# Pair loops of five layers written out, and one floor and reciprocal for both activation maxima of a quantised feed-forward

## What is computed

```python
x = x + cross_attention(ln(x), ctx)      # 16 heads, 256 keys
x = x + causal_attention(ln(x))          # 16 heads
x = x + quantised_ffn(ln(x))
x = x + single_head_cross(ln(x), ctx)
x = x + causal_attention(ln(x))          # 16 heads
x = x + experts(ln(x))                   # 32 routed and a shared one
```

```python
scale = 127.0 / clip(max(abs(x), axis=-1), 1e-5)
xq = clip(round(x * scale), -128, 127) / scale      # for x, and again for silu(gate) * up
```

## Time and profile before

| | us |
|---|---|
| median of 3 runs | 1245.86 |
| range of the runs | 1245.34 to 1248.54 |
| the profiled execution | 1246.51 |
| its span | 1244.7 |
| TensorE busy | 1181.4 |
| VectorE busy | 814.7 |
| ScalarE busy | 643.4 |
| GpSimd busy | 559.6 |

### The profile page before, as it was taken

One profiled execution on the slowest core, in us unless ns is written; L12 is line 12 of the kernel. 1 busy time (PEld: TensorE's weight loads), 2 busy tenths in 40 slices (PEclk: granted clock), 3 DMA queues, 4 the chain that ended last, 5 costly groups with the idle time before them and its releaser, 6 DMA issues.

```text
span 1244.7 us, 30235 instructions
## 1 busy us (share of the span) xinstructions
PE 1181.4 (95%) x9751; PEld 933.6 (75%) x9760; DVE 814.7 (65%) x1805; ACT 643.4 (52%) x1394; POOL 559.6 (45%) x833
## 2 busy tenths in 40 slices
PE   6899999989997778989998999999999999999998
PEld 4688888767775546777777888888888888888886
DVE  4688888867776888868899764444444544444444
ACT  4777677645555887545555434434333434343432
POOL 2144444667774444568885223232323233323232
PEclk9999999999999999999999999999999999999999
DMA  8200000000001001200000233333333433333331
GB/s 274 73 27 17 17 17 8 2 1 2 0 0 35 1 1 42 62 26 2 0 0 28 89 106 125 107 102 118 108 107 109 140 103 116 116 106 103 118 107 62
DMA packets 34041, 80.13 MB, mean 64 GB/s; under 512 B 4416, under 2 KB 12096, under 8 KB 33984
## 3 DMA queue, kind: packets, MB, share of 16 engines
q1 hardware_dynamic: 32800, 78.09, 19.4%
q10 hardware_dynamic: 1184, 1.31, 0.3%
HBM read 77.03 MB, written 2.36 MB: 64 GB/s over the span
## 4 chain that ended last, share of the span: by engine, by line
PE 78%; POOL 6%; DVE 6%; issue 5%; ACT 3%; DMA 0%; DVEq 0%; POOLq 0%; ACTq 0%; SPq 0%
PE ps L2448 10%; PE ps L2449 10%; PE ps L2447 10%; PE ps L444 5%; PE ps L2530 5%; PE ps L2529 5%; PE ps L2531 5%; PE ps L459 3%; POOL Kbd L1419 3%; PE ps L432 3%; PE ps L1095 2%; POOL Sm L1412 2%; PE ps L260 2%; PE ps L1065 1%; PE ps L1086 1%
## 5 line engine op out<-in xcount | busy, mean ns | idle before, releaser
L2816 POOL TENSOR_TENSOR sw<-sg,wb 128x512 f32<-128x512 f32 x136 | 176.5, 1298 | 386.6 <-ACT sg L2640 352.7
L2719 DVE TENSOR_TENSOR a<-sw,ps 128x512 f32<-128x512 f32 x136 | 93.5, 687 | 224.8 <-POOL sw L2816 224.5
L2645 ACT ACTIVATE ah<-a 128x512 fp32r<-128x512 f32 x136 | 85.9, 632 | 290.8 <-DVE a L2719 261.6
L2447 PE MATMUL ps<-Hh,wh 128*128 128x512 f32 x544 | 215.3, 396 | 0.0
L2448 PE MATMUL ps<-Hl,wh 128*128 128x512 f32 x544 | 214.4, 394 | 0.0
L2449 PE MATMUL ps<-Hh,wl 128*128 128x512 f32 x544 | 214.4, 394 | 0.0
L2723 DVE TENSOR_TENSOR al<-a,ah 128x512 fp32r<-128x512 f32 x136 | 95.6, 703 | 62.4 <-ACT ah L2645 59.3
L760 ACT ACTIVATE Pr<-ps,mx 128x256 f32<-128x256 f32 x256 | 104.2, 480 | 61.0 <-DVE mx L629 56.4
L2447 PEld LDWEIGHTS ps<-Hh,wh 128*128 128x128 f32 x544 | 101.9, 187 | 24.9 <-issue 0.8
L2449 PEld LDWEIGHTS ps<-Hh,wl 128*128 128x128 f32 x544 | 101.8, 187 | 24.9
L2448 PEld LDWEIGHTS ps<-Hl,wh 128*128 128x128 f32 x544 | 101.9, 187 | 23.6
(11 more groups left out here) (238 smaller groups left out, 2448.8 us busy)
## 6 DMA issues: line engine op xcount, KB each, us to landing
wb<-token_weights SPq DMA_DIRECT2D x64, 512.0 KB, 3.6
raw<-in_ew SPq DMA_DIRECT2D x66, 384.0 KB, 3.0
cT<-in_ctxT SPq DMA_DIRECT2D x16, 256.0 KB, 2.7
cx<-in_ctxT SPq DMA_DIRECT2D x15, 256.0 KB, 2.8
X<-in_x SPq DMA_DIRECT2D x1, 1536.0 KB, 7.2
wqkv<-in_wqkv SPq DMA_DIRECT2D x2, 768.0 KB, 5.2
raw3g<-in_wg SPq DMA_DIRECT2D x1, 1024.0 KB, 5.3
raw3u<-in_wu SPq DMA_DIRECT2D x1, 1024.0 KB, 7.4
```

The source lines that it names most:

```text
L2447: eng.matmul(ps[:, bank, :], wh[:, u, w], HhT[:, c, cols], start=(c == 0), stop=False)
L2719: eng.tensor_tensor(a[:, tt, :], sw[:, tt, :], ps[:, UB[tt], :], ALU.mult).then_inc(m_a, 1)
L2816: eng.tensor_tensor(sw[:, tt, :], sg[:, tt, :], wb[:, u, tt * UT:(tt + 1) * UT], ALU.mult).then_inc(m_sw, 1)
```

## The change

Five pair loops become Python loops: the same steps in the same order, i is a number, and there is no loop instruction. In the feed-forward the two maxima of a buffer lie side by side in one tile (column 0 for a, column 1 for h). `scale_both(i)` computes the floor and the reciprocal of the second maximum of pair i and of the first one of pair i+2 with one instruction each. It stands after the row maximum of pair i+2, where `front1` had its own, and what followed `amax2`'s maximum directly is gone. At the first two steps and at the last two it works on one column. Readers of the scales wait on the joint semaphores.

```diff
@@ long_pipeline, routed_pipeline, both pairs()
-    with eng.Fori(0, (NPAIR - 4) // 2) as j:
+    for j in range((NPAIR - 4) // 2):
...
-    with eng.Fori(0, (NPAIR - 6) // 2) as j:
+    for j in range((NPAIR - 6) // 2):
...
-        with eng.Fori(0, 5) as j:
+        for j in range(5):
...
-        with eng.Fori(0, 2) as j:
+        for j in range(2):
@@ quantised_ffn
-    am = sb("am3", [P, 2, 1]); ac = sb("ac3", [P, 2, 1]); sc = sb("sc3", [P, 2, 1]); dq = sb("dq3", [P, 2, 3])
-    am2 = sb("am32", [P, 2, 1]); ac2 = sb("ac32", [P, 2, 1]); sc2 = sb("sc32", [P, 2, 1]); dq2 = sb("dq32", [P, 2, 1])
+    am = sb("am3", [P, 2, 2]); ac = sb("ac3", [P, 2, 2]); sc = sb("sc3", [P, 2, 2])
+    dq = sb("dq3", [P, 2, 3]); dq2 = sb("dq32", [P, 2, 1])
@@ vector
-        def front1(i, u):
+        def row_max(i, u):
             eng.wait_ge(ln_h, base + i + 1)
-            eng.tensor_reduce(am[:, u, :], h[:, u, :], AX.X, ALU.max,
+            eng.tensor_reduce(am[:, u, 1:2], h[:, u, :], AX.X, ALU.max,
                               apply_absolute_value=True).then_inc(f_am, 1)
...
+        def inner_max(i, u):
+            eng.wait_ge(f_a, 2 * i + 2)
+            eng.tensor_reduce(am[:, u, 0:1], a[:, u, :], AX.X, ALU.max,
+                              apply_absolute_value=True).then_inc(f_am2, 1)
+
+        def scale_both(i, u):
+            c = slice(0 if within(i, 0, last) else 1, 2 if within(i, -2, last - 2) else 1)
+            if within(i, -2, last - 2):
+                eng.wait_ge(f_am, i + 3)
+            reach(eng, f_am2, i + 1)
+            reach(eng, f_dq, i + 1)
+            reach(eng, f_dq2, i - 1)
+            eng.tensor_scalar(ac[:, u, c], am[:, u, c], 1e-5, 1.0 / 127.0, ALU.max, ALU.mult).then_inc(f_ac, 1)
+            eng.wait_ge(f_ac, i + 3)
+            reach(eng, f_ar, i - 1)
+            reach(eng, f_r, i + 1)
+            eng.reciprocal(sc[:, u, c], ac[:, u, c]).then_inc(f_sc, 1)
...
-                amax2(i, u)
+                inner_max(i, u)
...
-                front1(i + 2, u)
+                row_max(i + 2, u)
+            if within(i, -2, last):
+                scale_both(i, u)
@@ scalar, round2
-            eng.wait_ge(f_sc2, i + 1)
+            eng.wait_ge(f_sc, i + 3)
...
-                           scale=sc2[:, u, :]).then_inc(f_ar, 1)
+                           scale=sc[:, u, 0:1]).then_inc(f_ar, 1)
@@ gpsimd, scale2
-            eng.wait_ge(f_ac2, i + 1)
+            eng.wait_ge(f_ac, i + 3)
...
-            eng.tensor_tensor(dq2[:, u, :], wsc[:, 2:3], ac2[:, u, :], ALU.mult).then_inc(f_dq2, 1)
+            eng.tensor_tensor(dq2[:, u, :], wsc[:, 2:3], ac[:, u, 0:1], ALU.mult).then_inc(f_dq2, 1)
```

More of the change, by code:

```diff
@@ L1512, in quantised_ffn @@
     f_g = sem(n + "g"); f_u = sem(n + "u"); f_sg = sem(n + "sg"); f_a = sem(n + "a")
-    f_am2 = sem(n + "am2"); f_ac2 = sem(n + "ac2"); f_sc2 = sem(n + "sc2"); f_dq2 = sem(n + "dq2")
+    f_am2 = sem(n + "am2"); f_dq2 = sem(n + "dq2")
     f_ar = sem(n + "ar"); f_at = sem(n + "at"); f_ate = sem(n + "ate"); f_o = sem(n + "o"); f_y = sem(n + "y")
@@ L1655, in mul @@
                                      op0=ALU.mult, op1=ALU.mult).then_inc(f_a, 1)
[L1657 to L1663, removed]
-            eng.wait_ge(f_ac2, i + 1)
-            eng.reciprocal(sc2[:, u, :], ac2[:, u, :]).then_inc(f_sc2, 1)
         def body(i, u):
@@ L1686, in first @@
         def first():
-            front1(0, 0)
+            row_max(0, 0)
+            scale_both(-2, 0)
             ln_dve(eng, L, 1, 1)
@@ L1691, in first @@
             ln_dve2(eng, L, 1, 1, f_r)
-            front1(1, 1)
+            row_max(1, 1)
+            scale_both(-1, 1)
             ln_dve(eng, L, 2, 0)
@@ L1766, in round1 @@
             eng.nop(nofuse=True)
-            eng.tensor_scalar(r[:, u, :], h[:, u, :], sc[:, u, :], ROUND, ALU.mult, ALU.add).then_inc(f_r, 1)
+            eng.tensor_scalar(r[:, u, :], h[:, u, :], sc[:, u, 1:2], ROUND, ALU.mult, ALU.add).then_inc(f_r, 1)
         def scales(i, u):
@@ L1772, in scales @@
             eng.nop(nofuse=True)
-            eng.tensor_scalar(dq[:, u, :], wsc[:, :], ac[:, u, :], None, ALU.mult).then_inc(f_dq, 1)
+            eng.tensor_scalar(dq[:, u, :], wsc[:, :], ac[:, u, 1:2], None, ALU.mult).then_inc(f_dq, 1)
         def scale2(i, u):
-            eng.wait_ge(f_ac2, i + 1)
+            eng.wait_ge(f_ac, i + 3)
             reach(eng, f_y, i - 1)
-            eng.tensor_tensor(dq2[:, u, :], wsc[:, 2:3], ac2[:, u, :], ALU.mult).then_inc(f_dq2, 1)
+            eng.tensor_tensor(dq2[:, u, :], wsc[:, 2:3], ac[:, u, 0:1], ALU.mult).then_inc(f_dq2, 1)
         def add_x(t, u):
```

## The result

In the same rounds the kernel before took 1246.66 us (median, 1245.34 to 1249.52) and the changed one 1240.77 us (1239.60 to 1242.19). The ratio is 0.9947, with a 95% interval of 0.9936 to 0.9958: 0.5% faster, more than the 0.3% that can be told from no change. The profiled execution has a span of 1239.0 us against 1244.7, so 5.7 us less; between the medians it is 5.9. The sum had 7.3.

The account below looks back on a forecast made before the run. TensorE was taken to bound all layers but the feed-forward, judged by VectorE with ScalarE close behind. Savings of 1.2 + 1.1 + 4.6 + 0 + 0.4 = 7.3 us gave 1238.6 us; range 1235.2 to 1242.4.

Parts of the forecast that it names:

- Cross attention and layer 2, 1.2 and 1.1 us: Twelve looped pairs in each layer, written out, save 0.10 us per pair in cross attention and 0.09 in layer 2.
- rival A: Outside the feed-forward TensorE hides the loops, so only 4.6 us go: 1241.2 us; 12%.
- rival C: Code loading shows: 44 kB per pair waited for in 12 cross pairs, 28 us, partly; near 1250 us or above; 3%.
- Feed-forward, 4.6 us: Feed-forward: over 13 periods the last second sg starts 4.6 us earlier, at 4.76 us per pair instead of 5.12.
- ScalarE's floor of 4.76 us: Feed-forward: ScalarE's steps per pair sum to 4.76 us, just below VectorE's written-out period of 4.85, and set the pace.
- Part 2: Feed-forward: one floor and one reciprocal for both maxima, worth 0 to 1.1 us within the 4.6.
- no gap ahead of VectorE's product ends with sg: Sign for the feed-forward: VectorE should show gaps ahead of the product that end with sg; two pairs take 9.5 us.
- the reserve: Feed-forward: 1.3 us left before the later joint scale would hold up ScalarE's ar.
- rival D: TensorE's half-clock stretches at joints between layers appear or go, up to 1.7 us each: 1236.9 or 1240.3 us; 12%, split.
- Layer 5, +0.4 us: Fifth layer, 10 looped pairs: 7.73 us each looped, 7.69 written out, so 0.4 us saved; range 0 to 2.6.
- this way to fail: The prediction fails if the measured written-out pairs were short for their place at a layer's end, not for being written out.

Follow-up runs that it names:

- VectorE's nudge: Changed kernel plus one extra one-element addition on VectorE ahead of hn, once, at pair 4 of layer 5; one pair took 8.69 us and the alternation went on.
- GpSimd's nudge: Changed kernel plus one extra one-element GpSimd addition, once, at pair 4 of layer 5; ratio 0.9940, layer 5 at 7.807 us per pair.

## Why the prediction was right, and where it was not

*Forecast and time.* 1238.6 us was forecast and 1240.77 measured, inside 1235.2 to 1242.4; faster, as was thought likely. Of the 2.2 us between them, 1.4 are in the saving (7.3 against 5.9 between the medians), and 0.8 is that the medians of before differ between the two sets of runs.

*Cross attention and layer 2, 1.2 and 1.1 us.* Measured 1.3 and 1.1, right to 0.1 us in both. In layer 2 that is partly luck: the looped pairs alternate between 7.84 and 7.69, 0.07 us per pair and not 0.09, and the remaining 0.36 us come from the first looped interval (8.05, now 7.69), which the prediction didn't look at. A written-out pair at the end of a stage, in which TensorE was full in both forms, was a sound measure of what the loop costs, and rival A (TensorE hides it) fell. Instruction loading shows as 1.05 MB on queue 8 (0.51 before) and as 2 and 3 GB/s beside TensorE rows that are full, and the intervals are those of the pair that was measured ahead of time: rival C fell too.

*Feed-forward, 4.6 us.* Measured 4.7. ScalarE's floor of 4.76 us, added up from five steps of the written-out pairs, came out at 4.754. Part 2 was said to be worth 0 to 1.1 us within this: it is 0.1, because VectorE at 4.85 doesn't use up its lead in the layer. The loops alone give 4.6 us, 0.92 per pass of two pairs. The 0.5 us in all that the Trainium skill's price of a compare-and-branch (Advanced Engine Details and Errata, Control Flow Timing) would make of them is not what this stage shows; the Trainium skill prices the branch alone. How the 0.92 us divide between the branch and the register arithmetic no run separates. Two readings of rows were loose: VectorE's looped stretch of 10.67 us holds 1.35 us of idle time, so its instructions don't follow each other almost without a gap, and the second product needs 0.72 us by the rows and not 0.77. Neither moves the sum. Two signs were wrong: no gap ahead of VectorE's product ends with sg, since h grew by 0.28 us where it meets GpSimd, and the reserve is 0.97 us. Alone, the joint scale would have given 3.3 of the 4.7.

*Clock, rival D.* One half-clock stretch more at one joint and one less at another, 1.25 and 1.2 us, so within the 1.7 us allowed for, and one at 652 us that cost next to nothing. In the fourteen traces such stretches come and go also where the code up to there is the same; one with few of them (the control with VectorE's nudge) saved 7.5 us in all though its layer 5 was the slowest but one. So the totals alone don't rank these kernels.

*Layer 5, +0.4 us: the step that failed.* The prediction took pair 14's 7.69 us as the price of every written-out pair. That pair is a single one at the layer's end, 7.67 to 7.70 in a steady state only if hn and Kbd keep their distance. The prediction had named this way to fail, written-out pairs that are short for their place at a layer's end, and gave it no price. For ten pairs in a row two rhythms were possible, and the one seen in four of the six traces with this layer written out on all engines in this order (two of the four have a nudge) is 0.11 us per pair longer than the loop. Where the layer is bound by TensorE with a little waiting, that waiting comes from a chain through three engines, and the length of an instruction on it depends on which of two engines begins first. I gave ends of 0 and 2.6 us and excluded a loss without a reason; the lower end had to be below nothing. The 14.94 of 15.46 us was the hint: with 3% of slack on the engine that is nearly the bound, other engines still decided when it waits, and that could go either way.

## What to carry to other kernels

A loop's price could be read from a written-out pair beside it where the bound engine was full in both. Where it waited a little, a pair's place in a repeating pattern mattered more than a branch. There it is worth trying to take the loop out engine by engine: here it gained on VectorE and GpSimd, and the gain was lost when TensorE and ScalarE were written out too. When two parts of a change lower the same floor, time each alone before keeping both; the joint scale brings 3.3 us with loops and 0.1 without them.

## What the runs showed of the hardware

- A VectorE tensor_scalar on 128x256 elements takes 0.41 us when no GpSimd instruction bars it, and otherwise lasts until 0.15 us behind the end of the GpSimd instruction that began before it, up to 1.02 us. (One exception: in the kernel with VectorE's nudge hn began at 568.84, in the last 0.05 us of the first half of Kbd, and ended at 569.62, 0.15 behind the end of the second half.) Begun ahead of Kbd, it makes the Kbd pair 1.41 to 1.44 us long and not 1.23. In four of the five long pairs of the changed kernel hn is late by 0.01 us or less.
- It goes the other way too: GpSimd's rs (128x1) takes 0.55 us, and 0.63 to 0.73 where VectorE's h, begun 0.18 to 0.08 us ahead, holds it up. Begun 0.08 ahead, h did so in two kernels at the pair where they settled and once at GpSimd's nudge, and didn't in the other pairs.
- In layer 5 the same written-out instructions have intervals of 8.00 and 7.66 or of 7.70 each. Both passages from the one to the other come at the pair in which h holds up rs; a push of one small GpSimd instruction held only for one pair.
- A looped pair costs 0.10 us in the cross attention, 0.07 in layer 2 (and 0.36 in its first one, 8.05 and not 7.69), nothing in the single-head layer, and 0.14 (with the joint scale, paced by ScalarE) to 0.46 us (without it, paced by VectorE) in the feed-forward, where 0.106 and 0.353 us per interval times 13 fall on ten looped pairs: the same loop instruction, by what the bound engine has beside it.
- TensorE's half-clock stretches at the joints lasted about 3.4 us, in the kernel with layer 5 looped once 10 (clock 0.50 from 382.1 to 392.2). The two at the joints around the feed-forward moved the time by 1.2 us each, the one at 652 us by next to nothing. The kernel with layer 5 looped had one from 269.4 us on and none at 51, the changed one the other way round, and the kernel with VectorE's nudge had none at 392.7; up to there the three have the same code.
